# Scores of a second attention layer made for two heads at a time, as 64-row matmuls in the two halves of the array

## What is computed

```python
# second attention: 16 heads of 64, 371 context rows as keys, 4 more as a second attention
q = split_heads(x @ Wq + lora_q); k = split_heads(org_ctx @ Wk + lora_k)
s = einsum('bhid,bhjd->bhij', q, k) * 64 ** -0.5
p = softmax(s, axis=-1)
o = einsum('bhij,bhjd->bhid', p, v)
# out = merge(o) + merge(attention of q with the 4 ipa rows); then @ Wo + bo
```

## Time and profile before

| | us |
|---|---|
| median of 3 runs | 1279.31 |
| lowest, highest run | 1274.37, 1279.42 |
| span of the profiled execution, first to last instruction | 1277.4 |
| median run less this span | 1.9 |
| TensorE busy | 1066.5 (83%) |
| VectorE busy | 948.8 (74%) |
| ScalarE busy | 567.6 (44%) |
| GpSimd busy | 268.6 (21%) |

### The profile page before, as it was taken

One profiled execution on the slowest core, in us unless ns is written; L12 is line 12 of the kernel. 1 busy time (PEld: TensorE's weight loads), 2 busy tenths in 40 slices (PEclk: granted clock), 3 DMA queues, 4 the chain that ended last, 5 costly groups with the idle time before them and its releaser, 6 DMA issues.

```text
span 1277.4 us, 23029 instructions
## 1 busy us (share of the span) xinstructions
PE 1066.5 (83%) x7860; PEld 746.0 (58%) x7860; DVE 948.8 (74%) x2024; ACT 567.6 (44%) x1276; POOL 268.6 (21%) x303
## 2 busy tenths in 40 slices
PE   0688888882979999854688988998897699999997
PEld 0577777771634555643367877777776455455553
DVE  5588888897398888697567777777776667776775
ACT  3366666672433343441455556555555233222220
POOL 1422222202245563001000000000000013433331
PEclk9899999995699999896799999999998699999999
DMA  5000000001112122320000000000000231112100
GB/s 190 1 2 2 1 0 0 0 1 66 64 48 84 58 96 67 110 71 28 6 1 2 2 2 1 1 0 1 1 1 1 100 129 64 64 64 72 70 1 29
DMA packets 9935, 47.82 MB, mean 37 GB/s; under 512 B 1513, under 2 KB 3313, under 8 KB 6930
## 3 DMA queue, kind: packets, MB, share of 16 engines
q1 hardware_dynamic: 9874, 47.03, 10.7%
HBM read 45.92 MB, written 1.11 MB: 37 GB/s over the span
## 4 chain that ended last, share of the span: by engine, by line
PE 33%; DVE 30%; issue 20%; ACT 9%; POOL 5%; DMA 2%; DVEq 1%; ACTq 0%; POOLq 0%
PE pb L1119 8%; PE pb L1134 7%; POOL qz L1227 5%; DVE ST L844 4%; DVE ST L855 3%; DVE nm L850 3%; PE pb L640 2%; PE pb L613 2%; PE pb L597 2%; DVE ST L847 2%; ACT ST L728 2%; PE pb L1424 2%; PE pb L576 1%; ACT V L711 1%; PE pb L570 1%
## 5 line engine op out<-in xcount | busy, mean ns | idle before, releaser
L1119 PE MATMUL pb<-xT,KT 128*128 128x448 f16 x1248 | 244.2, 354 | 2.7 <-DVE qz L1197 2.7
L1227 POOL TENSOR_TENSOR qz<-qz,Z 128x448 f32<-128x448 f32 x128 | 169.1, 1331 | 286.8 <-ACT qz L1166 197.5
L1119 PEld LDWEIGHTS pb<-xT,KT 128*128 128x128 f16 x1248 | 121.6, 98 | 119.6 <-DVE qz L1197 5.8
L613 PE MATMUL pb<-KT,qz 128*112 128x375 f16 (+1 forms) x768 | 171.8, 334 | 3.2 <-POOL qz L921 2.1
L640 PE MATMUL pb<-V,ST 125*112 125x32 f16 (+1 forms) x1536 | 127.0, 214 | 53.2 <-DVE ST L855 52.9
L1134 PE MATMUL pb<-V,KT 128*128 128x448 f16 x816 | 162.6, 357 | 8.9 <-DVE V L1206 8.9
L640 PEld LDWEIGHTS pb<-V,ST 125*112 125x112 f16 x1536 | 109.9, 133 | 71.3 <-DVE ST L855 47.2
L736 ACT ACTIVATE ST<-pb 125x336 f16<-125x336 f32 x256 | 113.6, 444 | 45.1 <-PE pb L623 42.5
L855 DVE SCALAR_TENSOR_TENSOR ST<-pb,ST 125x336 f16<-125x336 f32 x256 | 127.7, 499 | 6.0 <-ACT ST L736 5.4
L1134 PEld LDWEIGHTS pb<-V,KT 128*128 128x128 f16 x816 | 80.3, 99 | 86.3 <-DVE V L1206 10.5
L623 PE MATMUL pb<-identf,ST 112*125 112x112 f32 x768 | 125.8, 273 | 1.6 <-ACT ST L728 1.6
(11 more groups left out here) (196 smaller groups left out, 1594.0 us busy)
## 6 DMA issues: line engine op xcount, KB each, us to landing
ST<-in_moe SPq DMA_DIRECT2D x9, 1536.0 KB, 7.8
ST<-in_moe SPq DMA_DIRECT2D x8, 1024.0 KB, 6.8
Z<-wd_scratch SPq DMA_DIRECT2D x16, 448.0 KB, 4.4
ST<-in_ctxT SPq DMA_DIRECT2D x4, 750.0 KB, 4.9
ST<-in_gens SPq DMA_DIRECT2D x2, 768.0 KB, 4.7
ST<-in_lora SPq DMA_DIRECT2D x2, 624.0 KB, 8.7
ST<-in_w1q SPq DMA_DIRECT2D x1, 1024.0 KB
ST<-in_w1k SPq DMA_DIRECT2D x1, 1024.0 KB
```

Source lines behind the costliest of these rows:

```text
L613: mm = pe.matmul(SB_[st % 2][0:S, 0:L.keys], qz[:, bs % 2, qa, h, :], kT[bs % 2][qb][:, h // L.per_tile, 0:L.keys], start=(n == 0), stop=( ...
L1119: mm = pe.matmul(banks[m % len(banks)][:, 0:HT], MW[:, es % 2, qa, c:c + 128], xT[:, qb, k, half * HT:(half + 1) * HT], start=(i == 0), st ...
L1227: pool.tensor_tensor(tile, tile, wdB[:, es % 2, half * HT:(half + 1) * HT], ALU.mult)\
```

## The change

In the second attention the scores of heads h and h + 1 (h even) are made together by a new function. Its matmuls take 64 partitions of queries and keys instead of 128: the even head those of 0 to 63, the odd head those of 64 to 127, alternately, the even head into `SB_[0]`, the odd into `SB_[1]`. Each head still has three matmuls of 371 columns. The function stands at the even head, and at the odd head there is none. It waits for the exponential of head h - 1, where `scores(h)` waited for that of head h - 2 and `scores(h + 1)` for that of head h - 1. The first attention keeps `scores`; the other engines' programs are unchanged.

```diff
+            def scores_pair(bv, bs, h):
+
+                i, st = bv * H + h, bs * H + h
+                if h == 0:
+                    pe.wait_ge(g_free, front_done(L, bv, bs, "k"))
+                if st >= 2:
+
+                    pe.wait_ge(s["exp_done1"], i)
+                for n, (qa, qb) in enumerate(PARTS):
+                    for side in range(2):
+                        r = slice(64 * side, 64 * side + 64)
+                        mm = pe.matmul(SB_[side][0:S, 0:L.keys], qz[r, bs % 2, qa, h + side, :],
+                                       kT[bs % 2][qb][r, h // 2, 0:L.keys], start=(n == 0), stop=(n == 2))
+                        if n == 2:
+                            mm.then_inc(s["s_mm1"], 1)
+
...
                 for h in range(H):
-                    scores(bv, bs, h)
+                    if l == 0:
+                        scores(bv, bs, h)
+                    elif h % 2 == 0:
+                        scores_pair(bv, bs, h)
                     if bs or h >= 2:
                         turn(bv * H + h - 2, bs * H + h - 2)
```

## The result

The changed kernel takes **1298.41 us** (median of 4 runs, 1296.65 to 1298.96), the kernel before in the same job 1276.85 us (4 runs, 1274.37 to 1279.42). The medians are 21.6 us apart; the ratio on record, worked out over all these runs, is 1.0163, with a 95% interval of 1.0141 to 1.0185: slower by 1.6%, about 21 us. The profiled execution is 18.9 us longer than that of before. First the page's first line of the changed kernel, then two windows of its second attention (columns of rows 2): the stretch of rows 2, and its six middle batches. Behind them stand the six middle batches of the kernel before.

The account below looks back on a forecast made before the run. The second attention looks bound by TensorE, but in heads 0 to 9 TensorE waits for VectorE and ScalarE. Batches 9 + 2.5 + 2 = 13.5, plus clock 4, gives 17.5; 1279.3 + 17.5 = 1297 us, range 1284 to 1322.

Parts of the forecast that it names:

- The added wait: Second attention: even-head pairs wait for the exponential of head h - 1; 13.5 us over all batches at the present clock.
- P: TensorE time of one pair's scores: 0.47 + 0.27 = 0.74 us, bounds 0.47 and 1.22.
- the chain P + 4.45: Middle batches, heads 12 and 13: time from one pair to the next through the V unit and exponential, 5.19 us.
- L600's excursion: Price of entering and leaving a mode with fewer rows, read from L600's one-partition matmuls: 0.27 us.
- the variant of the rival: Pairs in the second attention: each step shows one weight load of 0.13, 3 x 0.13 per pair, landing near 1315.
- The middle batches: Six middle batches of the second attention, each 1.5 us longer: +9 us.
- The first and last batch: Second attention: first batch +2.5 us, bounds 0 and 2.9; last batch +2 us, bounds 0 and 3.5.
- The clock: Idle 2.2 us before head 2 lowers TensorE's clock: 0.7 in each of six batches, +4 us.
- Signs: Second attention: matmuls two by two, transpose after 0.5 to 0.8 us, waits over 50 us, batches 45.5 to 46.5, clock below 0.99.
- No overlap: Pairs' halves do not overlap, or weight loads show: P is 1.22, +24 us, so 1321; chance 0.20.
- Covered wait: The odd head's exponential ends before TensorE reaches the pair; 13 us saved, 1266; chance 0.08.
- Cancelling: Free excursions, covered first and last batches, no clock drop: middle batches about level, 1276 to 1285; chance 0.07.

Follow-up runs that it names:

- the wait alone: Kernel before, single heads on 128 rows; only the second attention's even heads wait for the exponential of head h - 1, not h - 2: 1294.07 us, ratio 1.0125.
- pairs on 128 rows: Changed kernel with operands of all 128 rows in the pairs, same places and wait: 1304.57 us, ratio 1.0192.
- filler before head 10: Changed kernel with eight unused 128-row matmuls ahead of the pair at head 10: 1291.09 us, ratio 1.0118.
- single-head kernel: Kernel before with 64-row scores in the second attention, one head at a time, old order and wait: 1304.51 us, ratio 1.0202.
- neither filler: Changed kernel with unused matmuls before head 10 alone, 1291.09 us, or before the pairs at heads 2, 4, 8, 10 and 14, 1303.63 us.
- three-bank kernels: Changed kernel with a third score bank, the old wait and one transposing bank: 1294.72 us; the same with 128-row matmuls in the pairs: 1295.30 us.

## Why the prediction was right

It held: 1298.41 us against 1297.0, inside the range, for the reason it gave. That the two times lie 1.4 us apart is partly luck. The prediction stood on 1279.3 us for the kernel before, whose fourth run brought its median to 1276.85; the difference was to be 17.5 us and is about 21. Point by point:

- **The added wait** set the time, as forecast: the wait alone is 16 of 21 us. What comes on top, the odd head's scores ahead of the unit, was in the forecast as P in the chain P + 4.45, and the overlap pays for it. The pair starts at heads 2, 4, 6, 8 and 10 were worked out as 6.87, 5.63, 5.34, 4.72 and 4.81 us apart and are 6.90, 5.63, 5.34, 4.72 and 4.81. The gaps after those were to be 8.0, 5.2 and 5.3 and are 7.87, 5.17 and 5.35. The batch was to be 1.5 us longer and is 1.44.
- **What a pair costs.** P was 0.74 us, from L600's excursion of 0.27; the stay measures 0.23, plus 0.09 where TensorE was running, so P is 0.70 to 0.79. That part of it lies on the transposes behind the pair I had not seen. The matmuls start two by two, each two less than 0.01 us apart. The section Key Properties of the Trainium skill's "TensorEngine Tiling (Array Packing)", which says that changing the mode drains the engine, agrees, and these runs put the price to it. The six weight loads of a pair don't show. The second two start 0.05 us after the first two matmuls and run under them, on the same rows: the variant of the rival that followed from the Trainium skill's "TensorE: Matmul & The Clock Gate", What overlaps and what doesn't, with a load shown at each step, cost nothing, and there the trace differs from the page. (By the prediction's own terms that variant adds 64 x 0.39 x 0.8 = 20 us and lands at 1317, not near 1315.)
- **The middle batches**, +9, measured +8.6.
- **The first and last batch**, +2.5 and +2, measured +1.9 and +3.3. The last was the least certain: I had no chain for it. With no front units, nearly every pair there waits 0.5 to 1.3 us, and 2.2 of the 3.3 us are there with the wait alone.
- **The clock**, +4, is the step that was wrong in place and low in size. The sum has 6.7 us for it. I put one small drop in each batch behind the idle time of 2.2 us before head 2. That idle time is there (1.85 us), but only one of four drops follows it and costs almost nothing; the three that cost are at heads 10 and 11, without idle time of that size before them. The place was not baseless: the one drop of the pairs on 128 rows (from 793.7 us) and two of those with the filler before head 10 do follow it. I had looked for low clocks behind waits only, and the single-head kernel has most drops with hardly any waits.
- **Signs.** Transposes at 0.61 us (0.5 to 0.8), middle batches of 45.7 to 45.9 us where the clock holds (45.5 to 46.5), granted clock 0.97 instead of 0.99 or more: as said. The wait behind the exponential is 47.1 us, and I had said over 50; it is longest at head 2 (1.85 us), as said, but then at heads 10 and 8 (1.04 and 0.95) and not at head 4 (0.85).
- **The rivals.** No overlap: refuted by the pairs on 128 rows. Covered wait: VectorE and ScalarE did not pull ahead, since the exponentials did not move. Cancelling: the excursion is not free.

**What stays open** is which property of the work at heads 8 to 11 draws the drops. Of the 26 drops in the middle batches of all these kernels 15 stand at heads 10 and 11, and ten behind or in idle time of 1.8 us and more. Those at heads 10 and 11 come with 64-row scores beside L584 (five in the single-head kernel, none when heads 8 to 11 have 128 rows, two when only these have 64), but two also come with the later wait alone, on 128 rows, and neither filler removed them all. Whether the chip lowers the clock for the half array left unused, for a pattern in time or for something else was not shown. No run shifted the same work in time, and each count is from one execution.

## What to carry to other kernels

Before two steps are joined, ask which buffer the second one must now wait for one step earlier, and compare, head by head, when the engine arrives with when that buffer comes free; here the timeline of the kernel before gave the new pace to 0.1 us up to head 10. Array time saved is worth something only in stretches that TensorE paces; a busy share of nine tenths doesn't say which these are. And a matmul that occupies half the rows should be tried for itself first: its price (0.23 us a stay, and here more clock drops) can be more than the overlap returns.

## What the runs showed of the hardware

- Matmuls on the two halves of the rows, into different banks, run at once: six of 371 columns in 0.61 us to the next instruction, 0.94 to 1.00 on 128 rows.
- A stay in the 64-row mode between 128-row work costs 0.23 us, of which 0.10 falls on the fp32 transposes behind it, and 0.09 more on entering from a running engine.
- The granted clock depends on more than idle time: with TensorE busy throughout, a kernel fell to the 1.2 GHz level in five of six batches, and in none once four of 16 heads were back on 128 rows (one profiled execution of each).
- Drops also follow idle time: all four of the three-bank kernels begin right behind an idle stretch of 1.85 or 1.86 us, on 64 rows as on 128.
- A loop body with 124 more matmuls came with stalls of 2.59 and 2.64 us where the loop begins anew; their cause is not shown.
